# A prologue done by groups of four tiles, with bins and layer norms moved to GpSimd

## What is computed

```python
x = x + xattn(layernorm(x), ctx, ctx, positions)
    # Q, K, V = projections with bias; 16 heads of 8
    # dist = sqrt(sum((pos_q - pos_k)**2)); bins = clip(int(dist / 5.0 * 32), 0, 32)
    # attn = softmax(Q K^T / sqrt(8) + dist_emb[bins]); out = (attn V) Wo + bo
x = x + ffn(layernorm(x))
    # gate = selu(x wi + bi) wo + bo;  top 2 of it, weights divided by their sum
    # h_e = selu(x exp_wi[e] + exp_bi[e]);  out = sum of w_e (h_e exp_wo[e] + exp_bo[e]), 8 experts
```

## Time and profile before

| | |
|---|---|
| median of 3 runs | 243.73 us |
| profiled execution: its own time, span of its instructions | 244.11 us, 242.4 us |
| TensorE busy, matmuls | 188.3 us (78%) |
| VectorE, ScalarE, GpSimd busy | 170.7, 132.5, 35.9 us |
| mean granted TensorE clock, as a share of full speed | 0.921 |
| moved by DMA | 31.56 MB in 40044 packets |

### The profile page before, as it was taken

The page is one execution under the profiler, slowest core; times in us unless marked ns, Lnnn a source line. Parts: engine busy times, 40 slices in busy tenths (PEclk is TensorE's granted clock), DMA queues, the critical chain, the costliest instruction groups (busy, mean ns, idle before and its releaser), DMA issues.

```text
span 242.4 us, 6706 instructions
## 1 busy us (share of the span) xinstructions
PE 188.3 (78%) x2766; PEld 152.4 (63%) x2767; DVE 170.7 (70%) x406; ACT 132.5 (55%) x246; POOL 35.9 (15%) x37
## 2 busy tenths in 40 slices
PE   0149642484989939998789999999984889999972
PEld 0126420354878839998779997666684145998962
DVE  6059898898786743688578966567899654777573
ACT  0049975963683330485238455999982034778200
POOL 8981800340000001000100010030000400000000
PEclk9999957587999975899999999999999599999999
DMA  4994069999999999099990000000000000000005
GB/s 71 231 271 97 0 189 246 289 321 242 302 387 349 253 277 388 36 190 283 393 190 3 5 3 0 4 1 3 0 0 0 0 3 0 4 1 3 0 3 173
DMA packets 40044, 31.56 MB, mean 130 GB/s; under 512 B 10957, under 2 KB 36813, under 8 KB 40014
## 3 DMA queue, kind: packets, MB, share of 16 engines
q1 hardware_dynamic: 36450, 29.74, 45.7%
q10 hardware_dynamic: 3564, 1.40, 2.7%
HBM read 23.53 MB, written 7.60 MB: 128 GB/s over the span
## 4 chain that ended last, share of the span: by engine, by line
PE 47%; DVE 14%; DMA 13%; ACT 11%; issue 6%; SPq 5%; POOL 2%; ACTq 0%; DVEq 0%; POOLq 0%
PE pair L1094 8%; PE pair L1135 6%; PE pair L1123 6%; PE pair L1108 5%; DMA BB<-bins_dram 5%; DMA X<-in_x_dram 4%; PE pair L1327 4%; PE pair L1311 3%; ACT GE L589 3%; PE pair L1210 3%; SPq L278 2%; ACT GR L590 2%; PE pair L1147 2%; DMA part_dram_k<-parts_k 2%; PE pair L1293 2%
## 5 line engine op out<-in xcount | busy, mean ns | idle before, releaser
L1094 PE MATMUL pair<-BD,OH 128*128 128x64 bf16 x768 | 29.6, 202 | 14.8 <-issue 8.3
L1094 PEld LDWEIGHTS pair<-BD,OH 128*128 128x128 bf16 x768 | 28.2, 104 | 17.2 <-issue 12.7
L565 ACT ACTIVATE XCT<-pair 128x512 f32<-128x512 f32 x32 | 17.5, 595 | 38.3 <-PE pair L1123 38.3
L560 ACT ACTIVATE CX<-CX 128x1024 f32<-128x1024 f32 x16 | 16.9, 1055 | 10.1 <-DVE CX L815 10.0
L774 DVE TENSOR_TENSOR X<-X,pair 128x128 f32<-128x128 f32 x16 | 4.6, 288 | 23.7 <-PE pair L1147 23.7
L812 DVE TENSOR_REDUCE mx<-pair 128x16 f32<-128x1024 f32 x16 | 19.6, 1222 | 1.3 <-PE pair L1108 0.6
L815 DVE TENSOR_TENSOR CX<-pair,mx 128x1024 f32<-128x1024 f32 x16 | 19.6, 1225 | 0.5
L408 POOL TENSOR_TENSOR rstd<-vare,half_neg 128x4 f32<-128x4 f32 x4 | 4.5, 1130 | 103.4 <-DVE vare L796 103.4
L1123 PE MATMUL pair<-ident,CX 128*128 128x128 f32 x128 | 18.3, 288 | 1.2 <-ACT CX L560 1.2
L1135 PE MATMUL pair<-VD,XCT 128*64 128x18 f32 x512 | 18.6, 216 | 0.0
L1108 PE MATMUL pair<-KS,QS 102*64 102x64 bf16 x512 | 18.4, 201 | 0.0
(11 more groups left out here) (199 smaller groups left out, 390.9 us busy)
## 6 DMA issues: line engine op xcount, KB each, us to landing
BB<-bins_dram SPq DMA_DIRECT2D x16, 512.0 KB, 9.7
KS<-part_dram_k SPq DMA_DIRECT2D x8, 384.0 KB, 7.3
QS<-part_dram_q SPq DMA_DIRECT2D x4, 768.0 KB, 11.5
w_ei<-in_L_ffn_exp_wi_dram SPq DMA_DIRECT2D x8, 256.0 KB
w_eo<-in_L_ffn_exp_wo_dram SPq DMA_DIRECT2D x8, 256.0 KB
w_ei<-in_fside_BxSx_dram SPq DMA_DIRECT2D x2, 768.0 KB, 10.0
part_dram_k<-parts_k SPq DMA_DIRECT2D x4, 384.0 KB, 5.9
part_dram_q<-parts_q SPq DMA_DIRECT2D x4, 384.0 KB, 5.8
```

The lines of the kernel that those rows point to most:

```text
L560: nc.scalar.activation(PR[:, t % 2], PR[:, t % 2], ACT.Exp).then_inc(exp_done, 1)
L565: nc.scalar.activation(PT[:, t % 2, 4 * half:4 * half + 4, :].rearrange("p c n -> p (c n)"), PTP[half][:, :], ACT.Copy).then_inc(pt_ev, 1)
L1094: mm(o, OH[:, t % 2, i * P:(i + 1) * P], BD[:, s], start=(i8_ == 0 and s == 0), stop=False, skip_group_check=True)
```

## The change

1. Position loads, distance, root, bins, their stores, statistics and norms are done for one group of four tiles at a time. VectorE does the bins of group 0, GpSimd those of groups 1 to 3 (`squares`, `bins`), in seven small steps after the root, where one comparison is two instructions.
2. The square root is `Ln` and then `Exp` with scale 0.5, both on ScalarE (`root`), for groups 2 and 3 inside the tile loop, at t = 2 and t = 5.
3. Both layer norms go to GpSimd (`layer_norm`, `layer_norm2`), with the bf16 parts of norm 2 (`split2`) and the scaling of the experts' output weights.
4. The constant bias rows are gone; `KS` and `QS` have 96 rows, and `KS` is set to zero in two halves.
5. Keys and queries have two PSUM banks each in turn, queries three part buffers; the first parts of the queries are stored as soon as they are there. The score products take the two batches innermost.
6. The context loads go partly through SyncE; the expert weights are loaded after the last bin block, their biases in tile 9's place. `CX`, `XN`, `XCT` lie in other buffers, and the output bias is added by groups.

The diff, cut to its core:

```diff
@@ SyncE
+            load_pos(0)
+            sp.dma_start(posq[:, :, :], pos.rearrange("b l c -> (b l) c").rearrange("(t p) c -> p t c", p=P)).then_inc(d_posq, 16)
+            load_x(0)
+            load_x(1)
+            load_cx(2)
+            load_x(2)
+            load_cx(3)
+            load_x(3)
+            for g in range(1, NG):
+                load_pos(g)
+            store_bins(0)
             store_parts("k", 0)
+            store_parts("q", 0, (0,))
+            spread_bins(0)
             stack_parts("k", 0)
+            store_parts("q", 0, (1, 2))
+            spread_bins(1)
+            stack_parts("q", 0)
             store_parts("k", 1)
             store_parts("q", 1)
+            spread_bins(2)
             stack_parts("k", 1)
+            store_parts("k", 2)
             stack_parts("q", 1)
             spread_bins(3)
+            store_parts("q", 2)
+            store_bins(1)
+            store_parts("k", 3)
+            store_parts("q", 3)
             for t in range(4, T):
                 spread_bins(t)
-                if t < TG + 2:
-                    store_parts("k", t - 2)
-                    store_parts("q", t - 2)
+                if t in (TG, 2 * TG):
+                    store_bins(t // TG + 1)
...
-                if t >= T - E:
...
+            for e in range(E):
+
+                sp.dma_start(w_ei[:, e, :], e_wi[e]).then_inc(d_ew, 16)
+                sp.dma_start(w_eo[:, e, :, :], e_wo[e].rearrange("(c p) h -> p c h", p=P)).then_inc(d_ew, 16)
@@ GpSimd
+            def inverse_std(g):
+
+                link(nc.gpsimd.tensor_scalar(vare[:, :], mv[:, tiles(g), 1], EPS, None, ALU.add))
+                link(nc.gpsimd.tensor_tensor(rstd[:, tiles(g)], vare[:, :], half_neg[:, :], ALU.pow))
+
+            def layer_norm(g):
+                pool.wait_ge(stats_ready, g + 1)
+                inverse_std(g)
+                if g >= 2:
+                    pool.wait_ge(xt_tr, g - 1)
+                for t in range(TG * g, TG * g + TG):
+                    last = nc.gpsimd.tensor_scalar(XN[:, g % 2, t % TG, :], X[:, t, :], mv[:, t, 0:1], rstd[:, t:t + 1], ALU.subtract, ALU.mult)
+                last.then_inc(xn_done, 1)
...
+            def squares(g):
+
+                ts = tiles(g)
+                pool.wait_ge(d_pos[g], 32)
+                link(nc.gpsimd.tensor_tensor(df[:, ts], posq[:, ts, :].unsqueeze(2).broadcast_to([P, TG, L, 3]), posk[:, ts], ALU.subtract))
+                link(nc.gpsimd.tensor_tensor(df[:, ts], df[:, ts], df[:, ts], ALU.mult))
+                link(nc.gpsimd.tensor_tensor(d2[:, ts], df[:, ts, :, 0], df[:, ts, :, 1], ALU.add))
+                link(nc.gpsimd.tensor_tensor(d2[:, ts], d2[:, ts], df[:, ts, :, 2], ALU.add))
+                nc.gpsimd.tensor_scalar(d2[:, ts], d2[:, ts], 1e-30, 64.0, ALU.max, ALU.min).then_inc(d2_clamped[g], 1)
+
+            def bins(g):
+
+                ts = tiles(g)
+                pool.wait_ge(root_done[g], 1)
+                link(nc.gpsimd.tensor_scalar(dv[:, ts], dv[:, ts], NB / MAX_DIST, float(NB), ALU.mult, ALU.min))
+                link(nc.gpsimd.tensor_scalar(rt[:, ts], dv[:, ts], 2.0 ** 23, -2.0 ** 23, ALU.add, ALU.add))
+                link(nc.gpsimd.tensor_scalar(dv[:, ts], rt[:, ts], MAX_DIST / NB, None, ALU.mult))
+                link(nc.gpsimd.tensor_tensor(sm[:, ts], dv[:, ts], dv[:, ts], ALU.mult))
+                link(nc.gpsimd.tensor_tensor(near[:, ts], sm[:, ts], d2[:, ts], ALU.subtract))
+                link(nc.gpsimd.tensor_scalar(near[:, ts], near[:, ts], 0.0, None, ALU.is_gt))
+                nc.gpsimd.tensor_tensor(binv[:, ts], rt[:, ts], near[:, ts], ALU.subtract).then_inc(bins_done[g], 1)
...
+            layer_norm(0)
+            layer_norm(1)
+            zero_keys(1)
+            layer_norm(2)
+            layer_norm(3)
+            pool.wait_ge(d_posq, 16)
+            squares(1)
...
+            bins(1)
+            pool.wait_ge(d_bo, 16)
+            for g in range(NG):
+                add_bo(g)
+            squares(2)
...
+            bins(2)
+            squares(3)
...
+            bins(3)
             for g in range(NG):
+                layer_norm2(g)
+                split2(g)
             pool.wait_ge(mv2_done, T)
             nc.gpsimd.memset(G1[:, :, :].rearrange("p t n -> p (t n)").bitcast(F32), 0.0).then_inc(g1_zero, 1)
+            pool.wait_ge(d_ew, 16 * 2 * E)
+            for i in range(2):
+                nc.gpsimd.tensor_scalar(w_eo[:, 4 * i:4 * i + 4], w_eo[:, 4 * i:4 * i + 4], SELU_SCALE, None, ALU.mult).then_inc(eo_scaled, 1)
@@ ScalarE
+            def root(g):
+
+                ts = tiles(g)
+                act.wait_ge(d2_clamped[g], 1)
+                nc.scalar.activation(dv[:, ts], d2[:, ts], ACT.Ln).then_inc(ln_done, 1)
+                act.wait_ge(ln_done, g + 1)
+                nc.scalar.activation(dv[:, ts], dv[:, ts], ACT.Exp, scale=0.5).then_inc(root_done[g], 1)
...
             evac_ct(0)
             evac_ct(1)
+            root(0)
...
             k_first(3)
             q_first(2)
+            root(1)
             evac_xt(3)
+            values(3)
             q_first(3)
...
                 if t >= 1:
                     aot(t - 1)
+                if t in (2, 5):
+                    root(2 + t // 5)
@@ VectorE
+            split("k", 0)
...
+            statistics(2)
+            split("q", 0)
+            split("k", 1)
+            statistics(3)
             split("q", 1)
+            split("k", 2)
             one_hot(0)
             split("k", 3)
             split("q", 2)
             one_hot(1)
+            split("q", 3)
@@ TensorE
-                for b2 in range(2):
-                    q0 = (t % TG) * P + b2 * L
-                    for c in range(HP):
-                        for ih in range(2):
+                for c in range(HP):
+                    for ih in range(2):
+                        for b2 in range(2):
+                            q0 = (t % TG) * P + b2 * L
...
+            x_transposes(3)
...
             biases(0)
+            project_q(3)
             scores(0)
             biases(1)
             scores(1)
```

More of the change, by code:

```diff
@@ L123, in build @@
         rest = sb("rest", [P, GTOK], F32, ab)
-        parts = {s: sb(f"parts_{s}", [P, 2, 3, GTOK], BF16, ab) for s in "qk"}
+        PBUF = {"q": 3, "k": 2}
+        parts = {s: sb(f"parts_{s}", [P, PBUF[s], 3, GTOK], BF16, ab) for s in "qk"}
         VD = sb("VD", [P, B, HP, VW], F32, ab)
@@ L215, in build @@
[L215 to L220, removed]
@@ L244, in build @@
         d_bb = [sem(f"d_bb{i}") for i in range(4)]
-        d_part = {s: [sem(f"d_{s}part{i}") for i in range(2)] for s in "qk"}
+        d_part = {s: [sem(f"d_{s}part{i}") for i in range(PBUF[s])] for s in "qk"}
         d_stack = {s: [sem(f"d_{s}stack{i}") for i in range(2)] for s in "qk"}
@@ L673, in _ @@
[L673 to L684 removed]
+                link(last)
@@ L685, in split @@
+                for t in range(TG * g, TG * g + TG):
+                    last = nc.vector.bn_aggr(mv[:, t, :], stats[:, t, :])
+                last.then_inc(stats_ready, 1)
+            def split(s, g):
+                hi, bias, done_r, done_m, done = ((k_hi, bcols[:, 1:2], k_r, k_mid, k_parts), (q_hi, bcols[:, 3:4], q_r, q_mid, q_parts))[s == "q"]
                 dve.wait_ge(hi, g + 1)
-                p3 = parts[s][:, g % 2]
-                nc.vector.scalar_tensor_tensor(out=rest[:, :], in0=bank[g][:, :], scalar=bias, in1=p3[:, 0, :],
+                p3 = parts[s][:, g % PBUF[s]]
+                nc.vector.scalar_tensor_tensor(out=rest[:, :], in0=KQB[s][g % 2][:, :], scalar=bias, in1=p3[:, 0, :],
@@ L746, in _ @@
-            last.then_inc(base_ready, 1)
             def one_hot(t):
@@ L1071, in project_q @@
                 pe.wait_ge(xt_ev, g + 1)
-                pe.wait_ge(k_r, g + 1)
-                mm(bank[g][:, :], w_q[:, :], XT[:, g % 2, :], start=True, stop=True).then_inc(q_mm, 1)
-            pe.wait_ge(wq_scaled, 1)
-            for g in range(2):
-                x_transposes(g)
-                project_q(g)
+                if g >= 2:
+                    pe.wait_ge(q_r, g - 1)
+                mm(KQB["q"][g % 2][:, :], w_q[:, :], XT[:, g % 2, :], start=True, stop=True).then_inc(q_mm, 1)
+            pe.wait_ge(ident_done, 1)
+            ctx_transposes(0)
+            ctx_transposes(1)
+            pe.wait_ge(d_wk, 16)
+            project_k(0)
+            x_transposes(0)
+            pe.wait_ge(d_wv, 16)
+            project_v(0)
+            project_k(1)
+            x_transposes(1)
+            pe.wait_ge(wq_scaled, 1)
+            project_q(0)
+            project_v(1)
+            ctx_transposes(2)
+            project_q(1)
+            project_k(2)
+            ctx_transposes(3)
+            project_v(2)
+            project_k(3)
+            x_transposes(2)
+            project_v(3)
+            project_q(2)
+            x_transposes(3)
             def biases(t):
```

498 lines of the change are left out of this document (188 added, 310 removed).

## The result

The changed kernel takes 258.25 us (254.77 to 260.62 in 4 executions), the kernel before on the same chip 243.84: a ratio of 1.049, with an interval of 1.040 to 1.058. It is slower by 5%; 241.5 had been forecast, and the range ended at 249. The profiled execution took 256.18 us with a span of 254.4.

The account below looks back on a forecast made before the run. Bound: first tile 0's start, then the DMA queue, then TensorE's 5 us a tile. Gains of 1.5 at tile 15 and 0.7 in the gate network, 2.2 us, took 244.1 to 241.9, median 241.5; range 230 to 249.

Parts of the forecast that it names:

- The two holes: TensorE idle before tiles 4 and 8, each hole ended by a bin block whose issue stood behind a bin store.
- the squares of group 1: GpSimd, before tile 0: starts after norm 3 ends at 31.5, takes 5.7 us, done at 37.
- Tile 0 at 50: Start of the tiles: transposes of tile 0 at 50 us, 11.5 earlier than before.
- Block 4 at 62: DMA queue: 12.1 MB from 19.5 us land tile 4's bin block at 60 to 64, taken as 62.
- Block 5 at 78, tile 4 at 86: Root, bins and store of group 2 ahead of block 5: 16.1 us after 62; tile 4 at 86, against 84.24.
- seven GpSimd instructions, 4.2: GpSimd's bins after a root: four one-input instructions at 0.5 us, three two-input ones at 0.7, 4.2 in all.
- Tile 5 at 91.6, tile 8 at 112.6: Step to tile 5 is 5.6 us; group 3's root and store ahead of block 9 then put tile 8 at 112.6.
- Tile 15 at 149.0: Last tile: 36.4 us after tile 8, so tile 15 comes 1.5 us earlier than before.
- Gate network and rest, 0.7 gained: After the tiles: ScalarE loses 5.8 us of norm 2 and parts, worth 0.7 us at the last group.
- rival three: GpSimd and VectorE hold each other, mainly in the gate network: 5 to 7 us, 247 us in all; chance 0.24.
- Score order at nothing, give or take 0.3 a tile: Score products: limited by their issue, so the new order counts nothing; without that cover, 0.3 us a tile either way.
- Nine table loads: ScalarE: a table load of 1.28 us before each logarithm and exponential, 3.4 us a root; nine loads in the trace.

Follow-up runs that it names:

- e10: e1 with a third buffer for the parts of the keys, in PT's second half: 240.26 us, ratio 0.982 to the kernel before.
- e11: e10 with root(1) on ScalarE behind its last projection copy instead of ahead of it: 237.91 us, ratio 0.975 to the kernel before.
- e1: The changed kernel with the bin stores of groups 2 and 3 moved later in SyncE's order, to the ends of tiles 7 and 11: 238.11 us, ratio 0.975.
- e2: The changed kernel with roots and bins of groups 2 and 3 made earlier, stores where they were: 241.20 us, ratio 0.985 to the kernel before.
- e4: The changed kernel with the scaling of the experts' output weights back on ScalarE: 255.96 us, ratio 1.050 to the kernel before.
- e6: The kernel before with only the change's order of the score products, the two batches innermost: 243.52 us, ratio 1.002.

## Why the prediction was wrong

The two holes, and the stores and roots that make them, were forecast; their size was not. The steps that failed are the way to the squares of group 1 (GpSimd done with norm 3 at 37.79 us, not 31.5), the price of GpSimd's one-input instructions (bins in 6.87 and 6.95 us, not 4.2, at each of the two holes), the rate of the transfers up to block 4, and TensorE's own work ahead of tile 8. Mark by mark:

- **Tile 0 at 50** (bounds 44 and 54): measured 57.38. The step that failed is GpSimd's: "ends norm 3 at 31.5, then the squares of group 1 ... 37". Norm 3 began at 32.18, behind the last statistics (32.09, where I had 28), took 5.6 us where I had 3 (its four instructions on X alone took 4.17), and ended at 37.79; the squares, priced right, ended at 43.70. Beside it I missed ScalarE's wait for the key buffer (8.14), which kept ScalarE from root 1 until 44.08; the two waits ended within 0.4 us of each other. e10 takes the second away and gains nothing, since root 1 then waits for the squares; e11 puts root 1 last, and tile 0 is at 49.59.
- **Block 4 at 62**: the block was issued at 62.12 and one-hot 4 made at 66.44, after 0.90 of waiting, so 4.4 later. The bytes were right (262 GB/s from 19.5 to 66.4 us is 12.3 MB, against 12.1); the rate was under both that I took, 271 and 298. That an earlier start is of no more use there, as forecast, shows in e11: tile 0 8.5 us earlier than in e1, one-hot 4 at 66.90 against 67.21.
- **Block 5 at 78, tile 4 at 86**: measured 85.36 (its one-hot) and 93.40. The mechanism (store ahead of block, root behind the copy) is the one I gave, and e1 and e2 show it. From one-hot 4 on I had 16.1 us; it took 18.9. The root was 3.44 (3.4 forecast). The mis-sized term is "seven GpSimd instructions, 4.2": 6.87 measured. I took 0.5 for a one-input instruction of 256 elements, from a cast of 128; they took 0.98 to 1.21.
- **Tile 5 at 91.6, tile 8 at 112.6**: measured 99.17 and 124.87. The step to tile 5 was 5.8 us (5.6 forecast). From there to tile 8 it is 25.7 where I had 21.0: 7.0 in place of 4.2 for the bins, and 7.6 in place of 5.2 from one-hot 9 to tile 8. That one-hot took 1.52 us, and my term ended with Exp, which was done at 123.05; TensorE's own products of the tile, up to the scores at 124.25, came after it.
- **Tile 15 at 149.0**: measured 162.74, 37.9 us after tile 8 (36.4 forecast). The 13.7 missing are 4.4 at one-hot 4, 2.8 and 4.7 at the two holes, 0.2 at tile 5 and 1.5 behind tile 8. With the 0.5 of the next item they are the 14.3 by which the profiled execution missed its 241.9; the median lies 2.1 higher still.
- **Gate network and rest, 0.7 gained, rival three**: 0.2 gained over all (91.66 against 91.87). The scaling took 11.05 us, not 6 to 9.6, and by e4 it cost 1.9 us, not 5 to 7. Of the times given, that rival's 247 was the nearest; its mechanism is not what made the kernel slow.
- **Score order at nothing, give or take 0.3 a tile**: 0.4 a tile in TensorE's busy time, nothing in the median (e6). The time was right, the reason wrong: as many products took 0.70 us in one order and 1.10 in the other, so that their issue did not limit them. Why the 0.4 did not come off the time is open (above).
- **Nine table loads**: right; one stands before the logarithm and one before the exponential of each root, 1.28 us each. The Trainium skill (ScalarE: Activation LUTs, "Table sets: the hidden batching unit") has one load for the two; the trace does not agree.
- **The bound itself**: I wrote of "first the start of tile 0, then the queue". e11 shows that the queue comes first: a start at 49.59 brings nothing while VectorE waits for blocks 3 and 4 until 58.57 and 66.90.

The chances failed in one way more. One price, that of GpSimd's one-input instructions, stands in the norms, in bins 2 and in bins 3, all on one chain. I let these terms err apart, when a single wrong row moved all of them the same way; slower deserved more than 0.29.

## What to carry to other kernels

An issue that waits holds everything behind it in its queue's order: before moving work to a slower engine, list for each store which loads of other data stand behind it, and put the store where its first reader is the next thing in the queue. Here two issues moved in one queue were worth 7%, while the one piece of work that was moved back by itself, the scaling of e4, was worth nothing that can be told. An early start is worth only what the next shared resource lets through, so ask for the second bound before counting the gain from lifting the first.

## What the runs showed of the hardware

- GpSimd's `tensor_scalar` on f32: about 0.9 us for 128 elements a partition with pointer operands (L400: 3.16 to 4.17 us for four), 0.98 to 1.52 us for 256, 5.5 us for 2048, while its `tensor_tensor` of 256 is 0.61 to 0.85. At 256 elements the two-input instruction was the cheaper one. GpSimd's groups in the changed kernel (busy us, mean ns of one | idle before):

```profile
L400 POOL TENSOR_SCALAR XW<-X,mv,rstd 128x128 f32<-128x128 f32 x16 | 14.6, 925 | 0.4
...
L490 POOL TENSOR_SCALAR w_eo<-w_eo 128x2048 f32<-128x2048 f32 x2 | 11.1, 5538 | 0.1
...
L423 POOL TENSOR_SCALAR w_eo<-w_eo 128x256 f32<-128x256 f32 x3 | 3.0, 986 | 0.2
...
L424 POOL TENSOR_TENSOR w_eo<-w_eo 128x256 f32<-128x256 f32 x3 | 1.8, 615 | 0.2
```

- Matmuls of 64 columns that alternate between the two halves of the output's partitions took 0.69 to 0.70 us for 32, and 1.10 when each half got sixteen in turn (e6 and the kernel before, above).
- TensorE's holes with no releaser lie inside the 48 bias products, and how many of those come behind the hole falls by about 3 a tile. TensorE's timeline in e1_store_late, tiles 4, 7, 10 and 11:

```profile
83.37 1.22 PE L1076 MATMUL pair<-BD,OH 128*128 128x64 bf16 x36 [1.88 <-issue]
...
102.35 0.98 PE L1076 MATMUL pair<-BD,OH 128*128 128x64 bf16 x28 [1.27 <-issue]
...
120.24 0.71 PE L1076 MATMUL pair<-BD,OH 128*128 128x64 bf16 x19 [0.63 <-issue]
125.48 0.64 PE L1076 MATMUL pair<-BD,OH 128*128 128x64 bf16 x16 [0.38 <-issue]
```

  The two longest, 3.82 and 2.12 us in the kernel before, lie where its DMA engines had a busy share of 1.09 and 1.06; but the first row here, 1.88 us, lies in a stretch (81.4 to 83.4 us) with a share of 0.22 and 35 GB/s. A tile issues some 123 matmuls and as many weight loads. The Trainium skill (Runtime: NRT & Kernel Launch, "Instruction fetch mechanics") says that an engine's program comes in blocks of 256 instructions over a DMA queue of its own; the step of about a tile agrees, and the 22 packets of the instruction queue with 0.36 MB, in the page of the changed kernel, are 16 KB each. That the fetch is late because the queues are full was not tested, and the row with a share of 0.22 speaks against it as the only reason.
